# Layer-0 attention of a four-layer graph network: sixteen summed rows a turn instead of twelve, GpSimd's signed blocks made as maximum times sign, three signed buffers

## What is computed

```python
h = jnp.maximum(_layernorm(x), 0.0)
s1 = jnp.einsum('bkf,ef->bke', h, W1)      # W1, W2: adj's two halves, e = 0..255
s2 = jnp.einsum('bkf,ef->bke', h, W2)
pre = s1[:, :, None, :] + s2[:, None, :, :] + b_lin
g = jnp.where(pre >= 0, pre, 0.2 * pre)
e = jnp.einsum('bije,e->bij', g, a) + adj
out = jax.nn.sigmoid(jnp.einsum('bij,bjf->bif', jax.nn.softmax(e, axis=2), h))
x = x + out
```

## Time and profile before

| | |
|---|---|
| median of 3 runs | 5407.69 us (5406.17 to 5408.93) |
| the profiled execution | 5412.65 us, its span 5410.9 us |
| busy: TensorE, VectorE | 5288.8 us (98%), 5225.0 us (97%) |
| busy: ScalarE, GpSimd | 5143.4 us (95%), 5080.7 us (94%) |
| granted TensorE clock | 0.996 of full |

### The profile page before, as it was taken

How to read it: one execution, slowest core, us unless ns; L and a number is a source line. 1 busy time by engine, 2 the same in 40 slices (tenths; PEclk the granted TensorE clock), 3 DMA queues, 4 the chain that set the end, 5 groups by cost and what they waited for, 6 DMA issues and landing times.

```text
span 5410.9 us, 115261 instructions
## 1 busy us (share of the span) xinstructions
PE 5288.8 (98%) x37702; PEld 2060.9 (38%) x37702; DVE 5225.0 (97%) x10763; ACT 5143.4 (95%) x13517; POOL 5080.7 (94%) x9752
## 2 busy tenths in 40 slices
PE   8999999999999999999999999999999999999997
PEld 2333333333333333333334333333333333333334
DVE  9999999999999999999999999999999999999993
ACT  8999999999999999999999999999999999999993
POOL 8899999999999999999999999999999999999990
PEclk9999999999999999999999999999999999999998
DMA  0000000000000000000000000000000000000000
GB/s 15 3 4 7 7 6 3 6 7 7 6 7 3 6 7 7 6 3 6 7 7 6 7 3 6 7 7 6 3 6 7 7 6 7 3 6 7 7 5 6
DMA packets 44381, 34.00 MB, mean 6 GB/s; under 512 B 4752, under 2 KB 39696, under 8 KB 43792
## 3 DMA queue, kind: packets, MB, share of 16 engines
q1 hardware_dynamic: 43792, 26.63, 1.6%
HBM read 9.84 MB, written 8.39 MB: 3 GB/s over the span
## 4 chain that ended last, share of the span: by engine, by line
PE 52%; ACT 26%; DVE 20%; issue 2%; DMA 0%; POOL 0%; SPq 0%; DVEq 0%; POOLq 0%
PE S L1163 29%; ACT ring L956 20%; PE R L1108 9%; DVE ring L751 8%; PE S L1108 5%; DVE ring L742 4%; PE W L1108 3%; DVE ring L746 2%; PE R L1301 2%; PE V L1108 1%; ACT h L1006 1%; DVE rh L890 1%; DVE gated L898 1%; DVE diff L894 1%; DVE h3T L902 1%
## 5 line engine op out<-in xcount | busy, mean ns | idle before, releaser
L956 ACT ACTIVATE ring<-V,U_minus 128x256 f32<-128x256 f32 x10681 | 4338.4, 850 | 1.6 <-issue 1.6
L1163 PE MATMUL S<-ring,a_window 128*32 128x512 f32 x29888 | 3401.9, 596 | 51.0 <-DVE ring L746 21.4
L620 POOL TENSOR_SCALAR ring<-W,U 128x256 f32<-128x256 f32 x6362 | 3175.7, 518 | 12.1 <-ACT V L982 11.8
L751 DVE TENSOR_TENSOR ring<-U,W 128x512 f32<-128x512 f32 (+1 forms) x2884 | 2536.1, 903 | 7.3 <-ACT V L982 7.3
L1163 PEld LDWEIGHTS S<-ring,a_window 128*32 128x32 f32 x29888 | 886.5, 109 | 2294.5 <-issue 2052.1
L610 POOL TENSOR_SCALAR signed<-W_signed,U_ceiling,U_floor 128x256 f32<-128x256 f32 x2880 | 1699.6, 594 | 6.3
L742 DVE SCALAR_TENSOR_TENSOR ring<-W,U,signed 128x256 f32<-128x256 f32 x2880 | 1193.8, 471 | 0.0
L746 DVE TENSOR_TENSOR ring<-U,W 128x256 f32<-128x256 f32 x1747 | 711.4, 409 | 0.0
L1108 PE MATMUL R<-mT,W 128*128 128x512 f32 (+1 forms) x640 | 334.9, 605 | 16.3 <-ACT mT L1068 16.3
L1108 PE MATMUL R<-AT,h 128*128 128x256 f32 x1264 | 311.9, 390 | 2.1 <-ACT h L1080 2.1
L582 POOL TENSOR_TENSOR rstd<-var,minus_half 128x4 f32<-128x4 f32 (+1 forms) x160 | 144.0, 900 | 141.2 <-DVE var L813 125.6
(11 more groups left out here) (185 smaller groups left out, 4512.9 us busy)
## 6 DMA issues: line engine op xcount, KB each, us to landing
X<-in_x SPq DMA_DIRECT2D x64, 128.0 KB, 2.1
X_held<-X SPq DMA_DIRECT2D x32, 256.0 KB, 2.3
out<-OUT SPq DMA_DIRECT2D x64, 128.0 KB, 1.9
edge<-in_L_gnn_w_w SPq DMA_DIRECT2D x3, 128.0 KB, 2.2
A<-in_adj SPq DMA_DIRECT2D x1, 256.0 KB, 2.7
Wn<-in_L_gnn_Wn SPq DMA_DIRECT2D x1, 128.0 KB, 2.9
Wm<-in_L_gnn_Wm SPq DMA_DIRECT2D x1, 128.0 KB, 3.0
weight<-in_L_gnn_u_w SPq DMA_DIRECT2D x2, 64.0 KB, 2.2
```

The source lines that it names most:

```text
L620: last = gp.tensor_scalar(ring[:, place, g, half * N:(half + 1) * N], W[:, y, c], LARGEST, U[:, y, c, i:i + 1], ALU.min, ALU.max)
L751: piece = dve.tensor_tensor(ring[:, place, g:g + groups].rearrange("p g (h j) -> p g h j", h=NB), u.unsqueeze(3).to_broadcast([P, groups, ...
L956: last = act.activation(ring[:, place, g, half * N:(half + 1) * N], W_scalar[y][:, c * N:(c + 1) * N], ACT.Relu, bias=U_minus[:, y, c, i:i ...
L1163: last = pe.matmul(S[y][g * ROWS:(g + 1) * ROWS, :], a_window[:, c, ROWS - 1 - row:2 * ROWS - 1 - row], ring[:, place, g], start=False, st ...
```

## The change

- The summed rows are 2, 6, 10, ... 30 (8 of 32) instead of 2, 7, ... 27 (6 of 32). On each side 56 lots a half turn remain instead of 58: 112 lots a turn instead of 116, of which 32 instead of 24 hold four summed blocks.
- A signed block is `max(W, U column)` times the column `sigma`, read from the plain `W` and `U`. `W_signed`, `U_signed`, `U_floor`, `U_ceiling`, `sigma_b0`, `sigma_limit`, and the semaphore `clamps_ready` are gone, with ScalarE's L976 and L979 and GpSimd's L599 and L600.
- There are three `signed` buffers instead of two.
- `FIRST_ROW` is (31, 29) instead of (0, 30), and the planner's table books 26 instead of 32 (tenths of a us) for `evacuate` on ScalarE and no longer 11 on GpSimd for each half turn. So the shares of all lots are dealt anew.

```diff
-SUMMED_EVERY, SUMMED_AT = 5, 2
-SUMMED_ROWS = [row for row in range(ROWS) if row % SUMMED_EVERY == SUMMED_AT]
-SUMMED_NODES = N // ROWS * len(SUMMED_ROWS)
-FIRST_ROW = (0, 30)
+SIGNED = 3
+SUMMED_COUNT = 8
+SUMMED_ROWS = [(2 * n + 1) * ROWS // (2 * SUMMED_COUNT) for n in range(SUMMED_COUNT)]
+FIRST_ROW = (31, 29)
...
-            put(scalar, PRE[h], half, norm=7.7, copy=2.7, evacuate=32)
+            put(scalar, PRE[h], half, norm=7.7, copy=2.7, evacuate=26)
...
-            if self.has_sums:
-                book(pool, half, 11)
...
-                    if turn.plan.has_sums:
-                        gp.tensor_scalar(U_floor[:, y], U_signed[:, y], sigma_limit[:], None, ALU.min)
-                        gp.tensor_scalar(U_ceiling[:, y], U_signed[:, y], sigma_limit[:], None, ALU.max).then_inc(clamps_ready, 1)
...
-                    if at == 0 and number >= 2:
-                        taken = divmod(number - 2, len(turn.plan.sum_lots))
+                    if at == 0 and number >= SIGNED:
+                        taken = divmod(number - SIGNED, len(turn.plan.sum_lots))
...
-                    i = turn.plan.signed_node(k, n)
-                    made = gp.tensor_scalar(signed[:, number % 2, at], W_signed[:, y], U_ceiling[:, y, i:i + 1], U_floor[:, y, i:i + 1], ALU.min, ALU.max)
+                    i = turn.plan.node(k, n)
+                    made = gp.tensor_scalar(signed[:, number % SIGNED, at], W[:, y, 1], U[:, y, 1, i:i + 1], sigma[:], ALU.max, ALU.mult)
...
-                    act.activation(U_signed[:, y].rearrange("p (b k) -> p b k", k=len(SUMMED_ROWS)),
-                                   side[y][:, N:2 * N].rearrange("p (b w) -> p b w", w=ROWS)[:, :, SUMMED_ROWS[0]:SUMMED_ROWS[-1] + 1:SUMMED_EVERY],
-                                   ACT.Identity, bias=sigma_b0[:], scale=sigma[:])
-                    act.activation(W_signed[:, y], W_bank[y][:, N:2 * N], ACT.Identity, scale=sigma[:])
```

More of the change, by code:

```diff
@@ L84 @@
 SETUP_REST = dict(vector_raw=12, transpose=14, vector_turned=20, product=24, vector_product=30, ready=34)
-DVE_CONST_A_WIDE, DVE_CONST_ALL = 5, 9
+DVE_CONST_A_WIDE, DVE_CONST_ALL = 5, 8
 DVE_REST_TURNED, DVE_REST_ALL = 6, 7
@@ L258, in node @@
         return half * P + g * ROWS + self.entry(t, n)[0]
-    def signed_node(self, t, n):
-        g, half = group_half(n)
-        return (half * GROUPS + g) * len(SUMMED_ROWS) + SUMMED_ROWS.index(self.entry(t, n)[0])
 PLANS = [Plan(turn) for turn in range(3)]
@@ L342, in gnn_stack @@
         sigma = sb("sigma", [P, 1])
-        sigma_b0 = sb("sigma_b0", [P, 1])
-        sigma_limit = sb("sigma_limit", [P, 1])
         AT_scaled = sb("AT_scaled", [P, NB, N])
@@ L369, in gnn_stack @@
         U_minus = sb("U_minus", [P, 2, EC, N])
-        W_signed = sb("W_signed", [P, 2, N])
-        U_signed = sb("U_signed", [P, 2, SUMMED_NODES])
-        U_floor = sb("U_floor", [P, 2, SUMMED_NODES])
-        U_ceiling = sb("U_ceiling", [P, 2, SUMMED_NODES])
-        signed = sb("signed", [P, 2, SIDE_BLOCKS, N])
+        signed = sb("signed", [P, SIGNED, SIDE_BLOCKS, N])
         W = sb("W", [P, 2, EC, N])
@@ L452, in gnn_stack @@
         pre_shift, h0_ready, h0T_psum, h0T_ready = (sem(n) for n in "pre_shift h0_ready h0T_psum h0T_ready".split())
-        clamps_ready, signed_ready = sem("clamps_ready"), sem("signed_ready")
+        signed_ready = sem("signed_ready")
         uw_psum, u_ready, w_ready, u_evacuated = (sem(n) for n in "uw_psum u_ready w_ready u_evacuated".split())
@@ L675, in setup_layer0 @@
                 dve.tensor_scalar(minus_b0[:], b0_scaled[:], -1.0, None, ALU.mult)
[L676 to L677 removed]
                 dve.wait_ge(pe_const, 1)
[L679 removed]
+                constant(dve.tensor_copy(AT[:], R0[:].rearrange("p (r i) -> p r i", r=NB)), 6)
                 dve.wait_ge(pe_const, 2)
                 dve.tensor_scalar(AT_scaled[:, 1], S[1][:, N:2 * N], -1.0, None, ALU.mult)
[L682 removed]
+                constant(dve.tensor_copy(AT_scaled[:, 0], S[1][:, 0:N]), 7)
                 constant(dve.tensor_copy(lin_w[:], R1[:, 0:P]), DVE_CONST_ALL)
@@ L742, in one_piece @@
                     piece = dve.scalar_tensor_tensor(ring[:, place, g, half * N:(half + 1) * N], w, U[:, y, c, i:i + 1],
-                                                     signed[:, number % 2, at], ALU.max, ALU.add)
+                                                     signed[:, number % SIGNED, at], ALU.max, ALU.add)
                 elif end - first == 1:
```

6 lines of the change are left out of this document (removed).

## The result

The changed kernel takes 7760.09 us (median of 4 runs, 7736.82 to 7763.86), against 5408.31 us for the kernel before on the same chip: 1.4336 of its time, with a 95% interval of 1.4305 to 1.4367 (the brackets behind later ratios are such intervals too; each ratio is to the kernel before on the same chip). The prediction was 5391 us. The profiled execution took 7736.82 us, its span 7735.0 us.

A forecast was written before the change was run, and what follows sets the result against it. VectorE was taken to set the pace, a turn being its work plus its idle time. The terms +44 +13 -53 -21 = -17 us took the profiled 5412.65 us to 5396, a median of 5391 us; range 5365 to 5440.

The forecast's parts named there:

- the price of the signed block: On GpSimd, maximum and multiply was taken at 0.53 us a block, between 0.455 from below and 0.605 from above.
- the fifth: Signed blocks above 0.56 us make GpSimd slowest, each 0.01 us more costing 1.28 us a turn; 5560 us at 0.605; chance 0.06.
- The rest of the sum: Whole run: VectorE's blocks +44, new wait +13, TensorE-related waits -53, contention -21, together -17 us.
- The wait for TensorE at the residual: VectorE's wait at L850, 40.3 us in all, goes because TensorE has fewer lots and VectorE comes later.
- The wait at the second elu: VectorE's wait for ScalarE at L818, 12.3 us, goes too, as it stands behind the same TensorE backlog.
- The new wait at lot 50: VectorE's summed blocks wait for GpSimd's signed block behind the addition of lot 47: 0.43 us a turn, 13 us in all.
- a new wait elsewhere: Sign of being wrong: VectorE newly waits for GpSimd anywhere but lot 50, above all at lots 2 and 66.
- VectorE's blocks: 32 more summed blocks and fewer pieces of one and two on VectorE: +1.5 us a turn, 44 us in the run.
- Contention: VectorE's two-input instructions wait less behind GpSimd's runs of plain blocks: -0.7 us a turn, -21 us, between 0 and -33.
- The third buffer: A third signed buffer changes nothing, 0 from either side, since GpSimd shows no wait for VectorE ahead of L610.
- It stays near 160.5 of a turn, with five us of room, so nothing: ScalarE's four more blocks against dropped L979 and L976 leave its load about unchanged: no effect on the time.
- the third rival: Lighter TensorE gives back more of VectorE's idle time, -60 instead of -53, no new wait, contention -33: 5359 us; chance 0.10.

The follow-up runs named there:

- the price list: Kernel before, with rows of four equal GpSimd instructions behind its last store, other engines idle: minimum-maximum takes 0.54 us each, maximum-multiply 1.20.
- the fast form: Changed kernel with a signed block's pair replaced by minimum, maximum on the same operands, three buffers, other numbers computed: 5337.83 us, 0.9880 of before.
- the last complete kernel: 16 summed rows, old signed blocks, changed kernel's table, two buffers; floor and ceiling made on GpSimd by multiply-add from `U`, no `U_signed`: 5404.89 us, 0.9963 of before.
- Breaking the runs alone: Kernel before with a one-column GpSimd memset ahead of the plain blocks of each lot without signed ones: 5399.66 us, 0.9988 of before.
- the fast form with two buffers: Changed kernel with minimum, maximum as a signed block's pair and two signed buffers instead of three: 5343.12 us, 0.9885 of before.
- the old chain by the same table: Changed kernel's plan and table, but signed blocks made as before the change (signed projections, clamps, minimum-maximum), two buffers: 5396.13 us, 0.9980 of before.

## Why the prediction was wrong, step by step

**The step that failed** is the price of the signed block: "I take 0.53, as the old one too has two operations and two columns", with 0.605 as the bound from above. It costs 1.20 (start to start in the price list, and 2.40 / 2 in the timeline of the changed kernel). 128 blocks a turn x 0.67 = 86 us; the forecast of 161.2 us for GpSimd's turn becomes 247, and the turn measured is 243.31, where GpSimd's plain blocks are also 0.02 us shorter each than in the fast form (485 ns against 504), 3 us a turn. The prediction named this sign itself: it is wrong "if the signed blocks take over 0.56 us". The bound was no bound: "the same distance over the signed block of today" rests on no row that shows an unlike operation. The trace gave no clear warning. The clamp L599, one operation on a fifth of the elements, takes 421 ns, nine tenths of a plain block's 455, but that alone doesn't tell a dear form from a short instruction: in the last complete kernel a multiply-add, a fast pair, takes 456 ns on 64 elements too.

The mechanism stood among the rivals, as the fifth: it decides from 0.56 us, each 0.01 us is 1.28 us a turn. By that, 0.67 us above 0.53 gives 165.1 + 1.28 x (120 - 56) = 247 us a turn. The threshold and the slope were right; the chance of 0.06 and the price of 5560 us were not.

By GPSIMD Engine Reference of the Trainium skill, section 3.1, a body with at most two operations for each element is bound by the ports. The trace of the kernel before could not contradict it, since its only two-column form is one of the fast ones. The price list does, and it decides: 0.8 ns for an element in minimum and maximum, 3.3 ns in maximum and multiply.

**The rest of the sum**, -17 us, is tested by the fast form with three buffers (the profiled execution is the slowest of its four, 5357.06 us). Its page:

```profile
PE 5214.4 (97%) x36742; PEld 2004.5 (37%) x36742; DVE 5187.2 (97%) x11035; ACT 5156.1 (96%) x13514; POOL 5122.9 (96%) x9631
...
L601 POOL TENSOR_SCALAR ring<-W,U 128x256 f32<-128x256 f32 x5401 | 2676.6, 504 | 10.9 <-ACT V L957 10.9
```

The addition of lot 47 from 500 to 5000 us, and all instances of L869 (before: L890), with min/median/max ns:

```profile
L616 POOL TENSOR_TENSOR edge_sum<-edge x28: 1278/1282/1290, 526.0 to 4956.4; 128x512 f32<-128x512 f32 x28
L869 DVE SCALAR_TENSOR_TENSOR rh<-tr,h3T x164: 426/861/1131, 301.5 to 5347.1; 128x512 f32<-128x512 f32 x156, 128x256 f32<-128x256 f32 x8
```

Its waits:

```profile
DVE rh L869 <- ACT tr L1046: 42.3, 12, 7.7
...
DVE diff L873 <- ACT cand L1052: 29.5, 34, 4.3
...
DVE ring L721 <- POOL signed L591: 29.5, 61, 0.5
```

Its timeline at lot 50, behind the addition:

```profile
2496.28 1.09 POOL L591 TENSOR_SCALAR signed<-W,U,sigma 128x256 f32<-128x256 f32 x2
2496.96 1.66 DVE L721 SCALAR_TENSOR_TENSOR ring<-W,U,signed 128x256 f32<-128x256 f32 x4 [0.50 <-POOL signed L591]
```

And 58 us later, around the masking of layer 2 (L839):

```profile
2553.68 1.21 DVE L839 TENSOR_TENSOR weight<-weight,AT 128x1024 f32<-128x1024 f32 x1
2555.42 1.66 DVE L721 SCALAR_TENSOR_TENSOR ring<-W,U,signed 128x256 f32<-128x256 f32 x4 [0.53 <-POOL signed L591]
...
2553.75 1.57 POOL L591 TENSOR_SCALAR signed<-W,U,sigma 128x256 f32<-128x256 f32 x1
```

The turn is 164.09 us, 1.6 less than before. The span is 5355.3 instead of 5410.9 us: -56, of which VectorE's busy time is -38 and its idle time -18. (With two buffers the span is 5337.7 and VectorE busy for 5186.2, idle time -34; the busy part is the same.) Predicted in the same terms: busy +44 - 21 = +23, idle 13 - 53 = -40. Point by point:

- The wait for TensorE at the residual goes, from 40.3 us to 3.2. Right. The wait at the second elu doesn't go with it (18.4 us, 12.3 before): it wasn't TensorE's backlog. L869's wait shrinks by 16 us, L873's grows by 10 (19.2 to 29.5).
- The new wait at lot 50 is 0.50 us; 0.43 was predicted. With two buffers it is the only one of its kind, 30 times, 14.8 us for the 13 of the sum. With three, VectorE waits 61 times, 29.5 us: in 26 turns it stands for another 0.53 us behind the masking of layer 2. There the masking stretches GpSimd's last signed block from 0.55 to 1.57 us, and the summed blocks behind the masking wait for it. That is a new wait elsewhere, one of the prediction's signs of being wrong.
- VectorE's blocks: their four groups add up to 4496 us of busy time, 26 more than before; 44 were predicted.
- Contention was sized too small. All else that VectorE does falls from 754 to 691 us, -64, where the sum had -21 and its bound -33: means of 890 ns for L869 at 128x512 (1037 before), 1303 for the masking of layer 2 (1520), 475 for the custom exponential (610). No L869 takes over 1.13 us, where under 1.5 had been forecast, but I had worked out one place only, where the runs of plain blocks held up others as well. Breaking the runs alone gave the whole shortening of L869 (23 us), but only 12 of these 64 us, as other instructions became longer; what else is in the 64 us, shifted neighbours above all, is argued from the masking's spread and not shown.
- The third buffer: 0 in time, right, though with two GpSimd waits 7.3 us for one.
- "It stays near 160.5 of a turn, with five us of room, so nothing" for ScalarE, and "covered" for GpSimd's clamps. From the fast form with two buffers to the old chain by the same table lie 0.95% (0.9885 to 0.9980, 51 us), which those instructions cost. The steps between are 0.21% (`W_signed`), 0.57% (clamps, with the semaphore and `W_signed` read) and 0.17% (`U_signed`); only the middle one is larger than its intervals. The last one also changes the form of the clamps. So work on engines with 3% of room wasn't free. That it counts because it stands at the start of a half turn, ahead of the first blocks, is argued only.

So the fast form would have been faster than forecast (5338 for 5391), 27 us below the range, and of the third rival's kind. Its sign was forecast, but not its make-up: the busy time was to rise by 23 us and falls by 38. That kernel computes something else, though: no pair of the fast four makes the signed maximum from plain `W` and `U` in one instruction. The complete version keeps `W_signed` and the clamps, and gets 0.37%.

## What to carry to other kernels

Never price an instruction by its kind: on GpSimd the exact pair of operations, and their order, decides over a factor of two, so measure a row of four behind the kernel's last store before building on it; where that can't be done, a form that no row shows needs a range far wider than the spread of the forms that rows do show: here it cost 1.20 us, twice the 0.605 that I had taken as the bound. A table of costs that deals out work must get the new price with the new instruction: told, this planner gave back three quarters of the loss. A shift of one cost moved the time by up to 0.7% at equal work, so a gain of a few tenths is to be compared under the same table.

## What the runs showed of the hardware

- On GpSimd, at 128x256 in float32 with two columns, (minimum, maximum), (multiply, add), (multiply, multiply) and (add, multiply) take 0.54 us and all other ordered pairs tried 1.20; one operation alone takes 0.90 us, more than a fast pair. A tensor_tensor multiply takes 2.72 / 4 = 0.68 us.
- A VectorE instruction with two inputs in SBUF was kept out by a run of plain blocks on GpSimd for longer than one block (1.39 us in the earlier trace rows, three blocks). SBUF — State Buffer of the Trainium skill, section "SBUF: two separate sides", has them exclude one another for an instruction; the runs here show that a one-column memset between the blocks shortens the wait (the longest L893 takes 1.50 us, against 1.97 before). It goes the other way too: a signed block beside VectorE's masking of 1.21 us took 1.57 us instead of 0.55.
- TensorE's mean granted clock fell from 0.996 to 0.920 in the changed kernel, where it was busy for 77% of the span; in the window above it stood at 0.91. TensorE is 1% of the chain that ended last, so that this cost next to nothing.
